# The carried state of a scan added by one product with the whole identity per tile, in place of four of 32 columns

## What is computed

```python
dt = softplus(dt @ dt_proj_w.T + dt_proj_b)        # (B, L, 512)
A = -exp(A_log)                                    # (512, 16)
def step(h, inp):
    dt_t, B_t, C_t, x_t = inp
    dA = exp(dt_t[..., None] * A)
    h = dA * h + (dt_t * x_t)[..., None] * B_t[:, None, :]
    y = einsum('bdn,bn->bd', h, C_t)
    return h, y
```

## Time and profile before

| | us |
|---|---|
| median of 3 runs | 686.33 |
| lowest and highest | 682.37, 688.09 |
| the profiled execution, whole | 687.74 |
| its span on the core, first to last instruction | 685.7 |
| PE busy in the span | 623.9 (91%) |
| DVE busy | 529.3 (77%) |
| ACT busy | 384.6 (56%) |
| POOL busy | 367.6 (54%) |

### The profile page before, as it was taken

How to read it: one execution, slowest core, us unless ns; L and a number is a source line. 1 busy time by engine, 2 the same in 40 slices (tenths; PEclk the granted TensorE clock), 3 DMA queues, 4 the chain that set the end, 5 groups by cost and what they waited for, 6 DMA issues and landing times.

```text
span 685.7 us, 26257 instructions
## 1 busy us (share of the span) xinstructions
PE 623.9 (91%) x11916; PEld 447.8 (65%) x11916; DVE 529.3 (77%) x487; ACT 384.6 (56%) x782; POOL 367.6 (54%) x132
## 2 busy tenths in 40 slices
PE   2999999589988999899999999999797999979997
PEld 1443445489977898777899889888644555535532
DVE  5894703769978998799889998987978668993446
ACT  1783666878766776678777777520164355323100
POOL 1000503579978898789889998980300235452000
PEclk9999999989999999999999999999998999999999
DMA  7990722600073100531341100016077999950203
GB/s 220 79 75 4 200 77 106 146 4 19 19 186 97 59 26 19 142 79 38 107 113 49 50 19 20 4 35 192 0 150 167 210 229 230 183 87 1 62 1 122
DMA packets 72631, 62.17 MB, mean 91 GB/s; under 512 B 34025, under 2 KB 57577, under 8 KB 72521
## 3 DMA queue, kind: packets, MB, share of 16 engines
q1 hardware_dynamic: 71560, 60.09, 39.4%
q10 hardware_dynamic: 960, 0.41, 0.2%
HBM read 44.22 MB, written 15.25 MB: 87 GB/s over the span
## 4 chain that ended last, share of the span: by engine, by line
PE 62%; DVE 8%; issue 5%; DMA 3%; ACT 3%; SPq 0%; DVEq 0%; ACTq 0%
PE PS L1135 31%; PE PS L1157 8%; PE PS L1274 4%; PE PS L1368 4%; PE PS L1384 4%; DMA patch_rows<-arena 3%; PE PS L1187 3%; PE PS L1154 2%; DVE mid L1772 2%; DVE X L1601 2%; PE PS L1253 1%; PE PS L1243 1%; PE PS L1349 1%; PE PS L1139 1%; DVE mid L1738 1%
## 5 line engine op out<-in xcount | busy, mean ns | idle before, releaser
L553 POOL TENSOR_TENSOR X<-X,spare 128x2048 f32<-128x2048 f32 x32 | 146.8, 4586 | 22.8 <-ACT mid L794 12.3
L1135 PE MATMUL PS<-mid,arena 128*32 128x128 f32 x4096 | 136.7, 273 | 7.0 <-issue 6.0
L1135 PE MATMUL PS<-WPR,arena 128*32 128x128 f32 x2048 | 132.3, 276 | 11.0 <-issue 5.0
L1135 PE MATMUL PS<-APROD,arena 128*32 128x128 f32 x2048 | 130.9, 276 | 4.2 <-issue 4.1
L1135 PEld LDWEIGHTS PS<-mid,arena 128*32 128x32 f32 x4096 | 121.2, 110 | 19.3 <-issue 13.5
L1135 PEld LDWEIGHTS PS<-WPR,arena 128*32 128x32 f32 x2048 | 113.8, 111 | 23.5 <-issue 16.0
L1135 PEld LDWEIGHTS PS<-APROD,arena 128*32 128x32 f32 x2048 | 112.1, 111 | 3.1 <-issue 2.9
L786 ACT ACTIVATE arena<-arena,small 128x512 f32<-128x512 f32 (+1 forms) x150 | 99.4, 711 | 19.3 <-DVE X L1601 10.3
L578 POOL TENSOR_TENSOR arena<-arena,PWR 128x512 f32<-128x512 f32 x30 | 43.3, 1472 | 70.7 <-PE PS L1274 70.6
L553 POOL TENSOR_TENSOR arena<-arena,spare 128x2048 f32<-128x2048 f32 x16 | 73.5, 4591 | 11.0 <-ACT mid L794 6.5
L553 POOL TENSOR_TENSOR WIN<-WIN,spare 128x2048 f32<-128x2048 f32 x16 | 73.4, 4588 | 8.3 <-DVE WIN L1601 5.5
(11 more groups left out here) (184 smaller groups left out, 1084.4 us busy)
## 6 DMA issues: line engine op xcount, KB each, us to landing
arena<-dt_rows SPq DMA_DIRECT2D x56, 256.0 KB, 4.1
arena<-patch_rows SPq DMA_DIRECT2D x40, 324.0 KB, 6.1
patch_rows<-arena SPq DMA_DIRECT2D x10, 648.0 KB, 7.8
X<-in_x SPq DMA_DIRECT2D x4, 1024.0 KB, 7.3
dt_rows<-arena SPq DMA_DIRECT2D x8, 512.0 KB, 5.1
spare<-c_rows SPq DMA_DIRECT2D x64, 64.0 KB, 2.2
tap_rows<-WPR SPq DMA_DIRECT2D x24, 88.0 KB, 8.0
mid<-dt_rows SPq DMA_DIRECT2D x8, 256.0 KB, 3.5
```

Source lines behind the costliest of these rows:

```text
L553: pool.tensor_tensor(HB[s % 4], HB[s % 4], CROW[:, k % 2:k % 2 + 1, :].broadcast_to([P, QN, HALF]), ALU.mult).then_inc(S["g_rd"], 1)
L1135: mm = pe.matmul(PS[32 * n:32 * n + 32, 4 + i, j * P:(j + 1) * P], DXT[:, DT_ * b + g, 4 * h + j, 32 * i:32 * i + 32], DIAGB[k % 2][n][:, ...
```

## The change

The four products that add the carried column, one for each group of 32 output partitions with 32 columns of the identity as weights, become one product whose weights are the whole identity and whose output is all 128 partitions of the column. It is marked as accumulating and as the last one of its group, as the four were.

```diff
                         if h and j == 0 and i % 2:
-                            for n in range(QN):
-                                pe.matmul(PS[32 * n:32 * n + 32, 4 + i, 0:1], IDENT[:, 32 * n:32 * n + 32], CARRY[:, DT_ * b + g, nq, i:i + 1], start=False, stop=True)
+                            pe.matmul(PS[:, 4 + i, 0:1], IDENT, CARRY[:, DT_ * b + g, nq, i:i + 1], start=False, stop=True)
                 mm.then_inc(S["u_ps"], 1)
```

## The result

The changed kernel takes 695.97 us (median of 4 runs, 691.39 to 696.37), the kernel before 685.58 us in the same series: ratio 1.0137, 95% interval 1.0092 to 1.0183, slower by 10.4 us. The profiled execution took 691.4 us, 689.3 of them the span. In a later series one run of the kernel before took 1268 us; it is left out of the ratios of that series.

A forecast was written before the change was run, and what follows sets the result against it. In the passes with h = 1, PE, DVE and POOL were all taken as almost full. PE's added 23.4 us less 9 covered gave near 15, so 686.3 + 14.7 = 701 us, range 692 to 711.

The forecast's parts named there:

- rival 3: Passes with h = 1: PE is not the bound, all stalls could shrink to nothing; +7, 693 us; chance 0.13.
- Removed, 0.06 us a place: inputs() with h = 1: eight one-column records cost 0.06 us; over 64 places removal gives at most 3.8 us of PE.
- Added, 0.20 + 0.31 + 0.02: Each of 64 places: leaving the narrow stream, whole product, bare narrow load; 0.36 us net, 23 us of PE.
- What is covered: Passes with h = 1: steps already held up absorb 4.8 to 13 us of PE's added time; 9 taken.
- Rival 1: The 64 places: the switch costs nothing, so at most 3.8 us of PE go; 682.5 us; chance 0.09.
- Rival 2: The 64 places: loads lie bare but nothing drains, 0.18 us a place; about 691 us; chance 0.08.
- Rival 4: Loop of inputs, scan, next inputs: nothing is covered, +23, 709.5 us; chance 0.15 together with a dearer place.
- What would show it: Trace after: 128 records, PEld waits 0.09 to 0.2 us both sides, inputs() 2.17 us, passes about 90 and 84 to 90.

The follow-up runs named there:

- the second pair of profiles: Changed kernel and kernel before run again with nothing changed, for a second profile of each: 694.33 us and 685.77 us.
- the added quartets: Kernel before with the four products of j = 1 issued twice (698.02 us) or three times (711.30 us) in each of the 64 places.
- the kernel that asked for 42: Kernel before with 12 more narrow one-column products in each of the 64 places, also the table's last row: 722.56 us, ratio 1.0588.

## Why the prediction was right, and where it was off

**The mechanism** held on PE's side: a whole product in a narrow stream stops it on entry, bares its loads and makes PE dearer. Forecast 701 us, slower by over 1%; measured 696, slower by 1.4% (0.9 to 1.8), within the range of 692 to 711. What becomes of that price in the time was forecast by another mechanism than the one found, and that the time fell within the range is in part luck: 696 lies nearer to rival 3's 693 than to 701.

**Removed, 0.06 us a place.** Right for PE's part (4.91 to 4.79 us a step without the carry). But it was taken for all that the removal can give, and 3.8 us were too little: without the carry the time falls by 8.0 us.

**Added, 0.20 + 0.31 + 0.02.** All three terms came out. A call with its state sum grew by 0.39 us against 0.36 or 0.365 summed; PE's need rose by 175.2 - 150.2 = 25.0 us where 23.4 were forecast. The 0.02 us a call left over may be that the four column groups run a little apart in the kernel before and are level after each stop; no run here tested it.

**What is covered** is the step that was mis-sized: 9 us were taken, the middle between 4.8 and 13. PE's need rose by 25.0 us and the passes by 11.2, so 13.8 were covered, just above the upper end. In the second pair of profiles it is 15.4. The upper end let a step be as long as before or longer, never shorter. But steps did get shorter: from first scan to first scan four steps of the first pass with h = 1 lasted 5.79 to 7.15 us before, and in the changed kernel all but one last 5.69 or less. The prediction asked whether a slower stream shortens the stalls in mid-stream and had no row for it. It does more than that: they are all but gone, 2.8 us and 0.5 us being left of about 16. Forecast were 23.4 - 9 = 14.4 us, the passes gave 25.0 - 13.8 = 11.2: the cover is what puts 701 too high.

**Rival 1** (no cost) and the page's fixed cost for small products, TensorEngine Tiling (Array Packing), section Instruction Overhead, in the Trainium skill: 24 records of one column take 0.18 us on PE when they are there in time, so four column groups together are not held to one product in 25 ns. But the prediction counted the eight records one behind the other, and they are two in each of four groups: 24 records are six in each group, 0.030 us apart, which is no less than the page's 25 ns. Read by column group the page and the traces don't contradict each other, and what the prediction refuted was its own count. **Rival 2** (loads without a drain) falls with the 0.20 us in front of each place. **Rival 3** (all stalls shrink to nothing, 693 us) is what came nearest for the cover: nearly all of the hold-ups went. Its name (PE isn't the bound) is wrong for the changed kernel, whose second pass PE alone sets. **Rival 4** (no cover) is refuted for this edit, but it is how the added quartets behave: 12.5 us of 14.1 and 27.4 of 28.2.

**What would show it.** inputs() at 2.17 us: 2.19. The passes at about 90 and 84 to 90 us: 90.8 and 87.2. 128 records: yes. PEld's wait at both sides of a place: only in front (0.20 us each, 6.3 us in the 32 places of a pass). Behind it the next load starts 0.02 us after the last one ends: with one moving column the loads are the work, so the drain doesn't appear as idle time there.

```profile
PEld PS L1138 <- issue: 6.3, 32, 0.2
```

## What to carry to other kernels

Price a product by the stream it stands in: four narrow ones side by side in a narrow stream cost 0.06 us of PE here, one whole product in their place 0.44, since it stops the stream once and bares its loads. Before you take a stall as fixed, ask whether it comes from the number of instructions: here, where PE is asked for some 35 records a us, an edit that adds time and takes records away got part of its price back, one that adds both in the same proportion paid nearly in full, and one that adds records faster than time paid more than three times its own part (38.7 us for 11.5). And look at the engine next in line before moving even 0.15 us onto it.

## What the runs showed of the hardware beyond that

PE's matmul records, each with a load beside it, never came faster than 33.9 a us over a pass; the kernel that asked for 42 got 32.1 and 33.5, and stood for up to 2 us at a time with nothing to wait for in the profile. The longest such stall of the kernel before in its passes with h = 1 lasts from 216.95 to 219.22 us; in the stretch 216.0 to 217.9 us of that trace one packet of the instruction queue is on its way:

```profile
q8 instruction: 1, 0.02, 4.4%
```

In the kernel before 21 such packets started in the first pass with h = 1, in the changed kernel 19, each 0.9 to 1.4 us long and of 16 KB. They are on their way in over a quarter of the time, so that one alone says little. But nearly all stalls of this kind end at the same distance behind such a packet. Here is the kernel before with 12 small products more, with one of its stalls and the packet ahead of it (in the stretch 418.7 to 419.8 us; it lands at 419.76):

```profile
421.23 0.20 PE L1142 MATMUL PS<-mid,cst 128*32 128x1 f32 x3 [0.73 <-issue]
```

```profile
q8 instruction: 1, 0.02, 5.3%
```

PE goes on 1.47 us after the packet has landed. Take as a stall any two matmul records that start more than 0.25 us apart. In the two passes of that kernel there are 48, and 46 of them end 1.2 to 1.62 us after such a packet has landed; a moment taken at random does so in 11 of 100 cases. With one quartet pair more it is 20 of 21 stalls, with two more 16 of 18, in the changed kernel with 12 small products more 11 of 11. With the carried state on DVE, where DVE sets the pace, it is 3 of 45, and in the kernel before, which has both kinds, 16 of 27.

One packet comes for 127 matmul records, whatever the edit: 94 for 11916 in the kernel before, 106 for 13452 in the one with 12 small products more. In that one they start 3.8 to 3.9 us apart on average and never less than 3.3, and 127 records in 3.8 us are 33 a us, the ceiling that was seen. So these stalls are waits for instructions: the times of the packets show it, and the kernels with more and with fewer records bear it out. Why the packets come no closer together is open. So is part of the last row of the table: the stalls make up 35 of its 45 us, the rest is in a slower pace without such a gap.
